# Perceiver kernel: maxima of head pair 1 made in the context stage, pair 2 of the attention without most of its maxima and with its row sums on VectorE

## The reference, cut to what matters

```
xn = layer_norm(ctx); ln = layer_norm(x)
q  = ln @ Wq * scale            # 8 heads of 64
k  = rope(xn @ Wk), v = xn @ Wv # 8192 keys, and 512 more from ln without rope
sim  = q . k                    # 512 x 8704 for each head
attn = softmax(sim)             # exp(sim - row maximum) / row sum
out  = attn . v @ Wo
```

## Time and profile before

| | us |
|---|---|
| median of three runs | 2217.95 |
| the three runs | 2217.94, 2217.95, 2218.29 |
| the profiled execution, its own time | 2220.97 |
| its span, first to last instruction | 2219.2 |
| TensorE busy | 2130.5 (96%) |
| VectorE busy | 1602.3 (72%) |
| ScalarE busy | 1102.6 (50%) |
| GpSimd busy | 918.0 (41%) |

### The profile page before, as it was taken

How to read it: one execution, slowest core, us unless ns; L and a number is a source line. 1 busy time by engine, 2 the same in 40 slices (tenths; PEclk the granted TensorE clock), 3 DMA queues, 4 the chain that set the end, 5 groups by cost and what they waited for, 6 DMA issues and landing times. The chain is left out here.

```text
span 2219.2 us, 37466 instructions
## 1 busy us (share of the span) xinstructions
PE 2130.5 (96%) x12720; PEld 1078.2 (49%) x12819; DVE 1602.3 (72%) x2346; ACT 1102.6 (50%) x1732; POOL 918.0 (41%) x643
## 2 busy tenths in 40 slices
PE   6899999989999999999899999999999999999977
PEld 3444444423333333333475665757566475755633
DVE  7677777659989899987565756667575666757673
ACT  4123323334444444555564655656465565647545
POOL 3335555459999999600222203122130222204045
PEclk9999999989999999999999999999999999999988
DMA  3445544433223322432323332342333334233413
GB/s 125 142 162 178 193 163 167 161 96 96 86 86 93 92 86 88 123 112 66 126 96 114 99 122 86 133 124 77 115 104 115 105 126 131 77 114 86 137 40 114
DMA packets 159854, 252.73 MB, mean 114 GB/s; under 512 B 11507, under 2 KB 63987, under 8 KB 159731
## 3 DMA queue, kind: packets, MB, share of 16 engines
q1 hardware_dynamic: 159730, 250.96, 35.3%
HBM read 211.73 MB, written 36.70 MB: 112 GB/s over the span
## 5 line engine op out<-in xcount | busy, mean ns | idle before, releaser
L67 PE MATMUL scores<-xt_hi,wt_hi 128*128 128x256 f16 (+3 forms) x1568 | 413.1, 275 | 10.9 <-DVE xt_lo L1503 5.2
L69 PE MATMUL scores<-xt_hi,wt_lo 128*128 128x256 f16 (+3 forms) x1568 | 412.9, 275 | 0.4
L68 PE MATMUL scores<-xt_lo,wt_hi 128*128 128x256 bf16 (+3 forms) x1560 | 410.3, 275 | 0.0
L1460 POOL TENSOR_TENSOR l_rstd<-l_var_eps,neg_half 128x1 f32<-128x1 f32 x71 | 67.0, 944 | 827.0 <-DVE l_var_eps L1514 827.0
L986 DVE TENSOR_REDUCE pmax<-mx 128x1024 f32 (+1 forms) x196 | 240.1, 1225 | 43.2 <-PE mx L1170 29.3
L69 PE MATMUL l_tok<-wt_hi,h_lo 128*128 128x512 f16 x576 | 218.4, 379 | 1.7
L1743 ACT ACTIVATE wt_hi<-stage 128x512 f16<-128x512 f32 x384 | 213.6, 615 | 8.8 <-DMA stage<-in_L_attn_Wf 8.8
L1183 PE MATMUL scores<-q_hi,res 128*128 128x512 f16 x544 | 209.4, 385 | 2.2 <-DMA res<-keys 2.1
L1184 PE MATMUL scores<-q_lo,res 65*128 65x512 f16 x544 | 208.3, 383 | 0.0
L67 PE MATMUL l_tok<-wt_hi,h_hi 128*128 128x512 f16 x512 | 194.1, 379 | 0.0
L68 PE MATMUL l_tok<-wt_lo,h_hi 128*128 128x512 bf16 x480 | 182.0, 379 | 0.0
(11 more groups left out here) (348 smaller groups left out, 4725.9 us busy)
## 6 DMA issues: line engine op xcount, KB each, us to landing
stage<-in_L_attn_Wf SPq DMA_DIRECT2D x60, 1024.0 KB, 5.3
keys<-wt_hi SPq DMA_DIRECT2D x136, 128.0 KB
res<-keys SPq DMA_DIRECT2D x68, 256.0 KB, 3.3
vb<-values SPq DMA_DIRECT2D x68, 256.0 KB, 5.6
stage<-in_ctx SPq DMA_DIRECT2D x16, 1024.0 KB, 10.1
values<-wt_lo SPq DMA_DIRECT2D x16, 1024.0 KB
stage<-in_L_ffn_f SPq DMA_DIRECT2D x16, 1024.0 KB, 5.3
res<-keys SPq DMA_DIRECT2D x68, 128.0 KB, 5.3
```

The costliest lines, as they stand in the source:

```text
L67: pe.matmul(out, lh, rh, start=first, stop=False, **kw)
L68: pe.matmul(out, lh, rl, start=False, stop=False, **kw)
L69: return pe.matmul(out, ll, rh, start=False, stop=last, **kw)
L1460: g.tensor_tensor(rstd[:, t:t + 1], var_eps[:, t:t + 1], k.neg_half[:, 0:1], ALU.pow).then_inc(rstd_done, 1)
```

## The change

Pair 1's maxima for groups 0 to 13 are made in the context (late units in every block from 1 to 15, group b - 1 in block b; block 15 keeps pair 0's group 15). The attention then makes in each pair p, in its first three groups, the units of pair p + 1 for groups 14, 15 and 16, and after them those of pair p + 2 for groups 0 to 13. So pair 2 has units in its first three groups only. GpSimd adds row sums for pairs 0 and 1 alone; pair 2's are VectorE's, as pair 3's are. `pair_max` moves from behind group 14 to behind group 2. `pmax` gets 34 columns a unit instead of 19. Four small DMAs a block are added in the context for the `km` buffers of pair 1 (blocks 2 to 13), and 12 loads of `km` fall away in the attention. At the attention's start one `load_m` moves behind the wait for the stores.

```diff
-MAX_COLS = KB + 2
+MAX_COLS = 2 * KB
+AHEAD = CTX_BLOCKS - 2
...
         def earlier_units(b):
-            return TT * b + (2 * TT if not isinstance(b, int) or b >= 3 else TT if b == 2 else 0)
+            return TT * (2 * b - 1) if not is_zero(b) else 0
...
         def late_pair(i, u):
             b = 2 * i + u
-            if isinstance(b, int) and b in (1, 2):
-                return b - 1, 1
-            return (b, 0) if isinstance(b, int) and b == CTX_BLOCKS - 1 else None
+            if is_zero(b):
+                return None
+            return (b, 0) if isinstance(b, int) and b == CTX_BLOCKS - 1 else (b - 1, 1)
...
                     load_km(u, u, 0)
-                    if is_first(i):
+                    if before_end(i, u, 2):
                         load_km(2 + u, u, 1)
...
-    CUT = [2 * TOK - P] * (PAIRS - 1) + [0]
+    CUT = [2 * TOK - P] * 2 + [0] * (PAIRS - 2)
...
         def max_block(p, b):
-            if isinstance(b, int) and b >= TURN:
-                return p + 2, b - TURN
-            return p + 1, b + 2
+            if isinstance(b, int) and b < KB - AHEAD:
+                return p + 1, b + AHEAD
+            return p + 2, b - (KB - AHEAD)
...
         def max_column(q, x):
-            return KB + x if q % 2 and isinstance(x, int) and x < 2 else x
+            return KB * (q % 2) + x
...
-                for b in range(2):
-                    load_m(1, b + 2, b)
+                load_m(1, AHEAD, 0)
                 for b in range(2):
                     load_v(0, b, b)
                 for u in range(2):
                     sp.wait_ge(k.stored[u], k.stores)
+                load_m(1, AHEAD + 1, 1)
...
-                for p in range(PAIRS - 1):
+                for p in range(2):
                     mine = slice(0, CUT[p])
...
-                pool.wait_ge(pool_summed, P_BUFS + (PAIRS - 1) * STEPS)
-                pool.sem_inc(pool_summed, STEPS)
+                pool.wait_ge(pool_summed, P_BUFS + 2 * STEPS)
+                pool.sem_inc(pool_summed, 2 * STEPS)
...
-                    with dve.Fori(0, TURN) as b:
+                    for b in range(KB - AHEAD):
                         block_work(p, b, False)
                     pair_max(p + 1)
-                    for b in range(TURN, KB):
+                    with dve.Fori(KB - AHEAD, KB) as b:
                         block_work(p, b, False)
```

More of the change, by code:

```diff
@@ L557, in _ @@
                     sp.wait_ge(km_in[u], KM_IN * HALF_BLOCKS)
-                    sp.wait_ge(km_in[2 + u], KM_IN)
+                    sp.wait_ge(km_in[2 + u], KM_IN * (HALF_BLOCKS - 1))
             @block.gpsimd
@@ L712, in key_high @@
                         act.wait_ge(km_in[u], KM_IN * i)
-                        act.wait_ge(km_in[2 + u], KM_IN)
+                        act.wait_ge(km_in[2 + u], KM_IN * i)
                     a.activation(kt[u][:, 0, tile, :], (a_cos, b_cos)[tile % 2][tile // 2], ACT.Copy).then_inc(k_hi_done, 1)
@@ L806, in late_unit @@
                             n, pair = late
-                            slot, loads = (2 + n, 1) if pair else (n % 2, HALF_BLOCKS)
+                            slot, loads = (3 - u, i + u) if pair else (n % 2, HALF_BLOCKS)
                             unit_max(earlier_units(b) + TT + j, pair, slot, j, loads if j == 0 else None)
@@ L883, in max_block @@
         def max_block(p, b):
-            if isinstance(b, int) and b >= TURN:
-                return p + 2, b - TURN
-            return p + 1, b + 2
+            if isinstance(b, int) and b < KB - AHEAD:
+                return p + 1, b + AHEAD
+            return p + 2, b - (KB - AHEAD)
         def max_memory(x):
-            if isinstance(x, int) and x < 2:
-                return x
-            return 2 if isinstance(x, int) and x == KB - 1 else x + 1
+            if isinstance(x, int) and x >= AHEAD:
+                return CTX_BLOCKS if x == AHEAD else x - 1
+            return x
         def max_column(q, x):
-            return KB + x if q % 2 and isinstance(x, int) and x < 2 else x
+            return KB * (q % 2) + x
         with nc.Block() as block:
@@ L990, in pair_max @@
                     if p:
-                        dve.wait_ge(mx_done, 1 + TT * (KB * p - 2))
+                        dve.wait_ge(mx_done, 1 + TT * (KB * (p - 1) + KB - AHEAD))
                         dve.wait_ge(rneg_done, p)
-                    first = 2 * (p % 2)
+                    first = KB * (p % 2)
                     v.tensor_reduce(rmax[:], k.pmax[:, :, first:first + KB], AX_X, ALU.max).then_inc(rmax_done, 1)
@@ L1252, in _ @@
                         row_sums(p - 1)
-                    with pe.Fori(0, (KB - 3) // 2) as i:
+                    for b in range(1, KB - AHEAD):
+                        block_steps(p, b)
+                    with pe.Fori(0, (AHEAD - 2) // 2) as i:
                         for u in range(2):
-                            block_steps(p, 1 + u, i)
+                            block_steps(p, KB - AHEAD + u, i)
                     block_steps(p, KB - 2)
```

## The result

The changed kernel takes 2263.27 us (median of four runs, 2260.97 to 2266.69) against 2217.94 (four runs of before by now): a ratio of 1.0208, 95% interval 1.0192 to 1.0224, so some 45 us slower. The forecast was 2260.5. The profiled execution has a span of 2264.9 us against 2219.2.

A forecast was written before the change was run, and what follows sets the result against it. TensorE, busy 96% of the span, was taken to bound the kernel. Terms 33.6 + 18.6 + 5.1 - 13.2 - 1.5 = +42.6 us on 2217.95 gave 2260.5 us, range 2232 to 2268.

The forecast's parts named there:

- The likeliest case: Normalise and GpSimd's weight pieces run together at context block boundaries: total 2247 to 2268 us, chance 0.56.
- the collision: Behind blocks 3, 5, ... 13, normalise slowed by GpSimd's pieces makes TensorE wait 3.1 us six times: +18.6 us.
- Late units: Context blocks 3 to 14: four late units each, 2.86 us more a block as in blocks 1 and 2: +33.6 us.
- the faster rival: Late units in the context cost only their matmuls, 1.28 us a block: 2214.5 us, chance 0.03.
- all four pieces go first: At the six boundaries GpSimd runs all its pieces before normalise, which starts 4.2 us late: upper bound 24.6 us.
- The clock: TensorE's clock falls behind three of the six boundary waits, 1.7 us each: +5.1 us, bounds 0 and 10.2.
- Pair 2: Attention's pair 2: 48 units fewer at 0.32 us, less 1.4 and 0.8 of VectorE and GpSimd sums: -13.2 us.
- The start: Attention's start: one load_m fewer ahead of load_v, so the values come sooner: -1.5 us, bounds 0 and -3.5.
- `pair_max`: Made earlier in the attention: one 0.3 us reduction in VectorE's order, its readers late anyway, put at nothing.

The follow-up runs named there:

- experiment 4: Changed kernel with normalise moved to the block's end ahead of late reduction 3, and late reduction 0 put ahead of low parts 0 and 1: 2218.86 us.
- Experiments 1 and 2: 1: changed kernel, normalise moved to the block's end ahead of late reduction 3, 2232.34 us; 2: changed kernel, GpSimd's 24 low-part pieces replaced by ScalarE zeros, 2233.52 us.
- Experiment 6: Changed kernel with pair 2's row sums split again between GpSimd (896 columns) and VectorE (128): 2277.59 us.
- Experiment 3: Changed kernel with two of GpSimd's four weight pieces left at each of six block boundaries, the other two written as zeros by ScalarE: 2243.9 us.
- experiment 8: Changed kernel with pair_max back behind group 14 and VectorE's loop cut anew: 2262.89 us.
- experiment 5: Kernel before with only the second load of keys at the attention's start moved behind the wait for the context's stores: 2212.42 us.

## Why the prediction was right, and where its terms were off

The likeliest case, the collision, is what happened: 2263.3 against 2260.5.

- *Late units:* +33.6 forecast, 35.7 measured. Block 14 without statistics took 0.6 us less as reckoned; the blocks in the loops took 0.2 us more each than blocks 1 and 2, which had not been foreseen. The reason given for the 2.86 us of a block was only half right: 1.0 us are waits, which experiment 4 ends by moving reduction 0 alone, and 1.85 us are TensorE's own time. So the lower bound, 15.4 with all waits gone, was too low; experiment 4 shows 22.2, and the faster rival, built on that bound, was out of reach.
- *The collision:* `normalise` 5.1 us forecast, 5.05 measured; waits 18.6 forecast, 18.7 measured. Experiments 1 and 2 remove it from both sides. The reading of the earlier trace rows that each `normalise` operation waits for most of one GpSimd operation, and not the reading that all four pieces go first, was the right one. (The 172.74 that the working calls the end of `normalise` in block 3 is its start; nothing in the sum hangs on it.) By the Trainium skill ("SBUF — State Buffer", section "SBUF: two separate sides") the shared port pair is an exclusive lock: whichever of the two operations starts first has it for the whole instruction, and the other fully blocks. Experiment 6 agrees: VectorE's sum of two SBUF operands starts at 898.51, 0.11 us behind GpSimd's operation, and ends at 900.63, 0.15 us behind its end.
- *The clock* was mis-sized: 5.1 us forecast, as half of six falls at 1.7 us. It fell behind all six, and for 1.6 us in three and 2.8 in three, 13.2 in all, outside the bound of 10.2. The steps that failed were to let it fall behind three of six only, and to take the one interval of block 0 as the price of each. Experiment 3 shows that behind 1.35 to 1.49 us it did not fall.
- *Pair 2:* -13.2 forecast, -16.06 measured, outside the bound of -15.4. The 48 units gave 48 x 0.323 = 15.5 us, as forecast, and 0.55 came from the wait of experiment 8 that is gone in pair 2 too. The two losses that the working took off, 1.4 us for VectorE's pace and 0.8 for GpSimd's last sums of pair 1, do not show. VectorE does take 2.27 us a step in the first three groups (the lines below), but TensorE keeps to its 2.18. VectorE begins these groups with time in hand and gets more while TensorE makes the row sums of pair 1, which take 1.0 us in either kernel; its lag reaches TensorE only at the twelfth and last unit, with 0.06 us.
- *The start:* -1.5 forecast, -6.25 measured, far outside its bound of -3.5. The first load's place was priced by its issue alone. In experiment 5, which has nothing else of the change, the first values are used 3.8 us earlier and the low clock behind the wait, 2.4 us, is gone: the same 6.2 us.
- *`pair_max`* had been put at nothing and gave 0.55 us in pair 1.

The start and pair 2 were 7.6 us too small as gains, the clock and the late units 10.2 too small as losses. That the total came within 3 us is luck in that part: four terms were off, and they cancel. The mechanism, the collision, and its price in waits are not luck.

VectorE in pair 2's second group (a unit's reduction, the sum, the next reduction), and TensorE's units of the same stretch:

```profile
853.03 1.22 DVE L987 TENSOR_REDUCE pmax<-mx 128x2 f32<-128x1024 f32 x1
...
854.16 1.22 DVE L1003 TENSOR_TENSOR h_lo<-h_lo,xt_lo 128x1024 f32<-128x1024 f32 x1
...
855.30 1.22 DVE L987 TENSOR_REDUCE pmax<-mx 128x2 f32<-128x1024 f32 x1
```

```profile
852.51 0.39 PE L1171 MATMUL mx<-km,q_hi 64*128 64x512 f16 x2
...
854.68 0.39 PE L1171 MATMUL mx<-km,q_hi 64*128 64x512 f16 x2
...
856.87 0.39 PE L1171 MATMUL mx<-km,q_hi 64*128 64x512 f16 x2
```

## What to carry to other kernels

Work moved between two stages that the same engine bounds pays at best its difference in price, and that can be negative, as here with 0.46 us a unit in the context against 0.32 in the attention; look then at what the moved work pushes aside in the other engines' orders. When an operation is put late in VectorE's order, look on GpSimd's timeline at the time where its followers will now fall: two groups that missed each other by 0.6 us can meet after the move. A wait of TensorE that cannot be avoided should be kept short: behind the six of 3 us the clock added 70% to their price here, and behind the six of 1.4 us nothing. And four terms that are each off can still add up to a good total, so each is to be compared with its own stretch of the trace.

## What had not been expected of the hardware

The low clock behind waits of nearly the same length (3.02 to 3.17 us) lasted for 1.6 or for 2.8 us of lost time, in turn from one odd block to the next, and it fell every time; behind the six of 1.35 to 1.49 us it never did. GpSimd's operations are hardly lengthened by the meeting (5.04 us instead of 4.50 for four), while VectorE's are (5.05 instead of 1.91). VectorE's reductions of TensorE's results are not: 1.21 us beside a GpSimd sum (692.34 in experiment 8), 1.22 in pair 2, where GpSimd has nothing to do. And two 128 KB loads took 3.19 us to issue where one took 0.60, so a load's issue time is no fixed price.
